# A five-layer decoder on one core: a table of step slots for each layer with projection halves apart, and the first batch requested ahead of the constant tables

## The reference, cut to what matters

```python
x = _layernorm(x + _L0_attn_ref(x, ...))            # layer 0: causal attention
x = _layernorm(x + _L0_xattn_ref(x, ctx, ...))      # layer 1: cross attention
x = _layernorm(x + _L0_ffn_ref(x, ...))             # layer 2: causal attention + 4 dense experts
x = _layernorm(x + _L1_attn_ref(x, ...))            # layer 3: attention with rotary positions
x = _layernorm(x + _L1_xattn_ref(x, ctx, ctx, group_prob, mask, ...))   # layer 4
x = _layernorm(x + _L1_ffn_ref(x, ...))             # top-1 routing to 8 experts
# in each attention layer:
q = h @ wq.T; k = h @ wk.T; v = h @ wv.T            # "projections"
scores = jnp.einsum('bhqd,bhkd->bhqk', q, k) * HD ** (-0.5)
attn = jax.nn.softmax(scores, axis=-1)
ao = jnp.einsum('bhqk,bhkd->bhqd', attn, v)
```

## Time and profile before

| | us |
|---|---|
| median of 3 runs | 1700.4 (1693.29 to 1702.75) |
| the profiled execution's own time | 1703.05 |
| its span, first to last instruction | 1701.3 |
| mean granted TensorE clock over the span | 0.941 of full |

### The profile page before, as it was taken

One profiled execution on the slowest core, in us unless ns is written; L12 is line 12 of the kernel. 1 busy time (PEld: TensorE's weight loads), 2 busy tenths in 40 slices (PEclk: granted clock), 3 DMA queues, 4 the chain that ended last, 5 costly groups with the idle time before them and its releaser, 6 DMA issues. The chain is left out here.

```text
span 1701.3 us, 29169 instructions
## 1 busy us (share of the span) xinstructions
PE 1514.3 (89%) x11260; PEld 1120.4 (66%) x11296; DVE 956.5 (56%) x2034; ACT 835.3 (49%) x1395; POOL 511.9 (30%) x690
## 2 busy tenths in 40 slices
PE   2799888988888999999999999987999999975997
PEld 2555655665555788787887877864655555545997
DVE  4455666755455342424335344367667788855886
ACT  0144445655444546455464564634543443435674
POOL 0024565531223111213223022033221223232766
PEclk9688989998888999999999999999999999987999
DMA  3645765755224021120210202223665354004542
GB/s 88 98 78 110 154 121 90 129 104 89 39 40 75 9 37 30 23 39 7 39 28 11 39 2 44 39 35 59 122 128 142 65 109 99 28 26 146 177 141 72
DMA packets 98745, 123.84 MB, mean 73 GB/s; under 512 B 8268, under 2 KB 88755, under 8 KB 96048
## 3 DMA queue, kind: packets, MB, share of 16 engines
q1 hardware_dynamic: 96096, 117.38, 35.1%
q0 software_dynamic: 1792, 3.94, 0.7%
q10 hardware_dynamic: 720, 0.66, 0.1%
HBM read 48.79 MB, written 9.51 MB: 34 GB/s over the span
## 5 line engine op out<-in xcount | busy, mean ns | idle before, releaser
L884 ACT ACTIVATE probs<-eslot 128x1024 f32<-128x1024 f32 x192 | 196.6, 1024 | 165.1 <-PE eslot L634 135.2
L1066 DVE TENSOR_REDUCE mx<-mslot 128x4 f32<-128x1024 f32 x128 | 156.5, 1223 | 155.4 <-PE mslot L608 154.9
L1302 POOL TENSOR_SCALAR_AFFINE_SELECT probs<-probs 128x512 f32<-128x512 f32 x128 | 83.4, 653 | 487.2 <-ACT probs L882 487.1
L1060 DVE TENSOR_REDUCE mx_blocks<-mslot 128x3 f32<-128x384 f32 x214 | 110.7, 551 | 193.9 <-PE mslot L608 182.4
L634 PEld LDWEIGHTS eslot<-stack 50*128 50x128 f32 (+1 forms) x1280 | 99.4, 192 | 119.1 <-issue 88.4
L634 PE MATMUL eslot<-stack 50*128 50x256 f32 (+2 forms) x1280 | 159.0, 328 | 17.2 <-ACT probs L884 9.6
L608 PE MATMUL mslot<-stack 48*128 48x256 f32 (+2 forms) x1110 | 142.2, 299 | 11.2 <-DMA stack<-split 9.6
L1274 POOL TENSOR_SCALAR ave<-amv 128x2 f32<-128x2 f32 x64 | 15.8, 247 | 432.2 <-DVE amv L983 342.6
L882 ACT ACTIVATE probs<-eslot 128x512 f32<-128x512 f32 (+1 forms) x256 | 111.7, 490 | 57.9 <-PE eslot L634 56.8
L648 PE MATMUL bank<-probs,v 128*32 128x256 f32 (+1 forms) x2048 | 137.4, 387 | 1.5 <-issue 1.5
L931 ACT ACTIVATE o<-bank 128x256 f32<-128x256 f32 x160 | 61.5, 384 | 115.3 <-PE bank L648 87.2
(11 more groups left out here) (226 smaller groups left out, 3381.7 us busy)
## 6 DMA issues: line engine op xcount, KB each, us to landing
stack<-split SPq DMA_DIRECT2D x240, 256.0 KB
w<-in_w SPq DMA_DIRECT2D x16, 1024.0 KB, 5.3
slot_rows<-hTf SPq DMA_DIRECT2D x4, 650.0 KB, 8.8
slot_rows_sb<-slot_rows SPq DMA_DIRECT2D x4, 650.0 KB, 6.3
expert_rows<-slot_rows SPq DMA_DIRECT2D x8, 260.0 KB, 2.8
xb<-in_x SPq DMA_DIRECT2D x8, 256.0 KB, 9.1
l<-in_l SPq DMA_DIRECT2D x2, 1024.0 KB, 9.0
qk<-in_ctx SPq DMA_DIRECT2D x8, 256.0 KB, 5.7
```

The costliest lines, as they stand in the source:

```text
L884: e = act.activation(PR[:, k, :, :, :].rearrange("p a k q -> p (a k q)"), ps[:, :, :, :].rearrange("p a k q -> p (a k q)"), ACT.Exp, scale ...
L1060: m = dve.tensor_reduce(MC[:, :, a, p], ps[:, 0:3 * P].rearrange("p (n k) -> p n k", k=P), AX.X, ALU.max)
L1066: dve.tensor_reduce(MX[:, :, :, p].rearrange("p q a -> p a q"), MSLOT[0][:, :, :].rearrange("p a (q k) -> p a q k", q=TT), AX.X, ALU.max)\
L1302: pool.affine_select(diagonal, diagonal, [[0, 2 * TT], [1, P]], ALU.is_ge, 0.0, base=0, channel_multiplier=-1)\
```

## The change

Four things are changed.

The table has new slots. The two halves of a projection, which stood in one slot in all layers, stand in different slots for `q` in layers 0, 2 and 3 and for `k` in layer 3. Of layer 0, `q` moves from -10 to -11, `q end` from -10 to -9 and `norm` from 28 to 32. Of layer 1, `H` moves from -13 to -15, `mask row` from -6 to -9, `xb` from -9 to -7, `y0` from 21 to 20. Of layer 2, `T` moves from -19 to -17 and `q end` from -16 to -15, `spread` from -11 to -10, `split` from -9 to -8, `yT` from 23 to 24, `route` from 29 to 30, `normf` from 37 to 38. Of layer 3, `T` moves from -19 to -17, `q end` to -15, `k end` to -13, `xb` from -10 to -13, `split` from -9 to -8, `stack` from -6 to -5, `v end` to -3, `yT` to 22, `w` from 26 to 24, `norm` to 30. Of layer 4, `keys` moves from -14 to -16, `masks` from -12 to -15, `turn masks` from -5 to -7, `stack` from -6 to -7, `xb` from -9 to -6, `v` from -3 to -4, `v end` to -2, `group` from 5 to 3, `scatter` from 38 to 35, `out` to 40. `H` of layers 2 and 3 stays at -20.

```diff
-        {"T": -13, "q": -10, "q end": -10, "k": -8, "k end": -8, "stack": -6, "v": -4, "v end": -4,
-         "shift": 8, "y0": 21, "y1": 21, "yT": 23, "w": 26, "w end": 26, "norm": 28},
+        {"T": -13, "q": -11, "q end": -9, "k": -8, "k end": -8, "stack": -6, "v": -4, "v end": -4, "shift": 8,
+         "y0": 21, "y1": 21, "yT": 22, "w": 26, "w end": 26, "norm": 32},
...
     EXP_LAG = (11, 11, 11, 11, 11)
-    MIX_LAG = (2, 1, 2, 1, 1)
+    MIX_LAG = (1, 1, 1, 1, 1)
```

```diff
+    EARLY = [(cols, "cols"), (tokens, "tokens"), (rope_cos, "rope_cos"), (rope_sin, "rope_sin"), (rope_swap, "rope_swap")]
+    SMALL = [(head_sum, "head_sum"), (head_spread, "head_spread"), (gate, "gate"), (prefer, "prefer"), (prefer_e, "prefer_e"),
+             (wg, "wg")]
...
         @block.sync
         def _(sp):
-            sp.dma_start(Y[:, 0, 0:P], t["causal_q"]).then_inc(consts_in, 16)
-            sp.dma_start(Y[:, 0, P:2 * P], t["upto"]).then_inc(consts_in, 16)
-            for dst, name in CONSTS:
-                sp.dma_start(dst.ap(), t[name]).then_inc(consts_in, 16)
-            sp.wait_ge(consts_in, 16 * (len(CONSTS) + 2))
+            sp.dma_start(X[0], t["x"][0:1].rearrange(flat)).then_inc(*x_in[0]())
+            sp.dma_start(ident[:, :], t["ident"]).then_inc(ident_in, 16)
+            for kind in "qkv":
+                sp.dma_start(WEIGHT_OF[kind][:, :, :], t["proj"][:, PROJ[kind](0), :, :]).then_inc(*weight_in[kind](0))
+            sp.dma_start(rows[:, 0, :], t["rows"][:, VROW[0], :]).then_inc(*row_in[0](0))
+            sp.wait_ge(ident_in, 16)
+            sp.wait_ge(consts_in, 16 * (len(EARLY) - 1))
+            sp.wait_ge(small_in, 16 * len(SMALL))
+
+        @block.scalar
+        def _(act):
+            act.dma_start(Y[:, 0, 0:P], t["causal_q"]).then_inc(tables_in, 16)
+            act.dma_start(Y[:, 0, P:2 * P], t["upto"]).then_inc(tables_in, 16)
+            for dst, name in EARLY:
+                act.dma_start(dst.ap(), t[name]).then_inc(tokens_in if name == "tokens" else consts_in, 16)
+            act.wait_ge(ident_in, 16)
+            act.activation(ident_b[:, :], ident[:, :], ACT.Copy)
 
         @block.gpsimd
         def _(pool):
+            for dst, name in SMALL:
+                pool.dma_start(dst.ap(), t[name]).then_inc(small_in, 16)
...
-            for k in range(RING):
-                dve.memset(QKS[k][:, :, 0, :].bitcast(F32), 1.0)
-                for a in range(2):
-                    dve.memset(QKS[k][HALF * a + 32:HALF * a + HALF, :, 1, :].bitcast(F32), 1.0)
+            for k in range(2):
+                dve.memset(QKS[k][:, :, :, :].bitcast(F32), 1.0)
...
             elif step == "k":
+                if l in (0, 2, 3):
+                    pe.wait_ge(*act_read.at("T", u))
                 project("k", u, source(u), 0)
...
+        pool.memset(QKS[2][:, :, :, :].bitcast(F32), 1.0).then_inc(*stack_ones(2))
```

More of the change, by code:

```diff
@@ L123, in schedule @@
     PLACE = (
-        {"T": -13, "q": -10, "q end": -10, "k": -8, "k end": -8, "stack": -6, "v": -4, "v end": -4,
-         "shift": 8, "y0": 21, "y1": 21, "yT": 23, "w": 26, "w end": 26, "norm": 28},
-        {"context": -17, "context sums": -14, "H": -13, "centre": -13, "T": -12, "TC": -11, "q": -10, "q end": -10, "mask": -10,
[11 rows of a table removed]
-         "turn masks": -5, "v": -3, "v end": -3, "group": 5,
-         "shift": 8, "y0": 21, "y1": 21, "yT": 23, "w": 26, "w end": 26, "norm": 28, "even": 30, "xT": 30, "even rows": 31,
-         "logits": 32, "chances": 33, "rank": 34, "scatter": 38, "out": 38},
+        {"T": -13, "q": -11, "q end": -9, "k": -8, "k end": -8, "stack": -6, "v": -4, "v end": -4, "shift": 8,
+         "y0": 21, "y1": 21, "yT": 22, "w": 26, "w end": 26, "norm": 32},
+        {"context": -17, "H": -15, "context sums": -14, "centre": -13, "T": -12, "TC": -11, "q": -10, "mask": -10,
+         "q end": -10, "mask row": -9, "k": -8, "k end": -8, "xb": -7, "stack": -6, "v": -4, "v end": -4, "shift": 8,
[7 rows of a table added]
+         "norm": 30},
+        {"keys": -16, "masks": -15, "T": -13, "q": -10, "q end": -10, "k": -8, "k end": -8, "turn masks": -7,
+         "stack": -7, "xb": -6, "v": -4, "v end": -2, "group": 3, "shift": 8, "y0": 21, "y1": 21, "yT": 23, "w": 26,
+         "w end": 26, "norm": 28, "even": 30, "xT": 30, "even rows": 31, "logits": 32, "chances": 33, "rank": 34,
+         "scatter": 35, "out": 40},
     )
     EXP_LAG = (11, 11, 11, 11, 11)
-    MIX_LAG = (2, 1, 2, 1, 1)
+    MIX_LAG = (1, 1, 1, 1, 1)
     for u in range(UNITS):
@@ L303, in attention_layers @@
     consts_in = semaphore("consts_in")
+    ident_in = semaphore("ident_in")
+    tokens_in = semaphore("tokens_in")
+    tables_in = semaphore("tables_in")
+    small_in = semaphore("small_in")
+    stack_ones = signal("stack_ones")
     experts_in = semaphore("experts_in")
@@ L330, in shift_rows @@
         return first, first + SHIFT
-    CONSTS = [(ident, "ident"), (rope_swap, "rope_swap"), (head_sum, "head_sum"), (head_spread, "head_spread"), (rope_cos, "rope_cos"),
-              (rope_sin, "rope_sin"), (cols, "cols"), (gate, "gate"), (prefer, "prefer"), (prefer_e, "prefer_e"), (wg, "wg"),
-              (tokens, "tokens")]
+    EARLY = [(cols, "cols"), (tokens, "tokens"), (rope_cos, "rope_cos"), (rope_sin, "rope_sin"), (rope_swap, "rope_swap")]
+    SMALL = [(head_sum, "head_sum"), (head_spread, "head_spread"), (gate, "gate"), (prefer, "prefer"), (prefer_e, "prefer_e"),
+             (wg, "wg")]
     EXPERTS = [(up0, "up0"), (l1, "l1"), (l2.ap(), "l2"), (downs, "downs"), (down3.ap(), "down3"), (l3.ap(), "l3"),
                (up3, "up3"), (up1a, "up1a"), (up1b.ap(), "up1b")]
+    flat = "b p t c -> (b p) t c"
     with nc.Block() as block:
@@ L364, in _ @@
             dve.memset(CLEAR[:, TOKEN:WIDE], 1.0)
-            dve.wait_ge(consts_in, 16 * (len(CONSTS) + 2))
+            dve.wait_ge(tokens_in, 16)
             for b in range(B):
@@ L368, in _ @@
                 dve.memset(XR[b][:, :, TOKEN + 1:WIDE], 0.0)
+            dve.wait_ge(tables_in, 32)
             dve.tensor_copy(upto_b[:, :], Y[:, 0, P:2 * P])
-            dve.tensor_copy(ident_b[:, :], ident[:, :])
             dve.tensor_copy(causal_q[:, :], Y[:, 0, 0:P])
@@ L1390, in stack @@
                 sp.wait_ge(*exp_filled.at(u - RING, PAIRS - 1))
+            elif u == 2:
+                sp.wait_ge(*stack_ones.at(2))
             for j, (a, b) in enumerate(zip(Q_PARTS, K_PARTS)):
@@ L1431, in reload @@
             sp.dma_start(WEIGHT_OF[kind][:, :, :], t["proj"][:, PROJ[kind](l), :, :]).then_inc(*weight_in[kind](l))
-        sp.dma_start(X[0][:, :, :], t["x"][0:1].rearrange(flat)).then_inc(*x_in[0]())
-        for kind in "qkv":
-            reload(kind, 0)
         reload("w", 1)
-        reload_row(0, 0)
         reload_row(1, 1)
```

1 line of the change is left out of this document (removed), and 18 rows, old and new, of the table PLACE.

## The result

The changed kernel takes 1602.15 us (median; 1590.84 to 1603.82), the kernel before 1697.41 us in the same comparison. The ratio is 0.9427 with a 95% interval of 0.938 to 0.9474: 5.7% faster, 95 us by the medians.

The account below looks back on a forecast made before the run. PE was taken as the bound, busy 89% of the span, with idle waits and a lowered clock in three stretches. Terms -13 - 14 - 28 - 10 + 5 = -60 took 1703.05 to 1643 us, range 1612 to 1686.

Parts of the forecast that it names:

- the clock term: PE work lost at 1.2 GHz: 6 of 25.1 us back in layer 0, 15 of 26.6 between layers 1 and 2, 3 of 8.7 in layer 3.
- The opening, -13: Kernel start: fewer DVE memsets and requests on POOL let PE start at 11.6 to 12.5 us, not 25.53; 13 us saved.
- Layer 0, -14: Layer 0: query bank read one slot later, after the `stack` landing; 8 us of idle time and 6 of clock saved.
- The limit that I saw close by: Layer 0: five slots from `stack` to the next query bank read, transfers 13 us, so 8 slots take at least about 21 us.
- Layers 1 to 2, -28: Between layers 1 and 2: later `T` removes PE's 12.9 us of waits for POOL's h, plus 15 us of clock.
- Layer 3, -10: Layer 3: `parts` before `split` saves 7 of 10.5 us of PE's waits, plus 3 us of clock.
- the waits only move on: Rival, all three turns: next limits close behind bring the old waits back; about -21 us, 1682 us; chance 0.22.
- Layers 2 and 4, 0: Layer 2's own 545 us stretch and layer 4, where PE is nearly always busy: no change, 0 us.
- What may cost, +5: Layers 0 and 2: `MIX_LAG` 1 leaves one slot for POOL's clearing between `exp` and `mix`; 5 us lost over 64 mixes.
- The rival in which POOL gates `mix`: Layers 0 and 2: POOL's 2.44 us blocks delay PE, 78 us in place of 5; 1716 us; chance 0.05.
- the one in which DVE's memsets hold up POOL's requests: Opening: POOL's six requests wait until 10.2 us, PE starts at 21, gain 4.5, and waits move; 1699 us; chance 0.03.
- more than forecast: Rival, whole kernel: waits gone and clock at 2.4 GHz throughout; -13 - 29 - 39 - 19 = -100, 1603 us; chance 0.07.

## Why the prediction was right and wrong

The direction, the places and, but for one in layer 3, the mechanisms held; the sizes did not, and they erred on one side. The step that failed is the idle time of PE, of which the sum counted too little; the clock term, though wrongly reasoned, was nearly right in size.

Between the two profiled executions 112 us went, where the sum had 60. Of these, 47 are PE's busy time and 65 its idle time; the sum had 24 (6, 15 and 3) for the clock and 36 for the rest (13, 8, 12.9 and 7, less 5). But the two lie apart on the clock. By the prediction's own sum, (1 - clock) x span, the clock gave back 100.4 - 46.1 = 54 us between them, and 91.6 - 62.5 = 29 us between executions near the medians (0.946 over 1696 us and 0.961 over 1602; an estimate). So of the 95 us by the medians the clock has about 29, and its term of 24 was nearly right. The idle time has the miss of some 29 us: 40 us in the three stretches where the sum had 28 less 5, 11 us in layers 2 and 4 (13.6 to 9.8 and 14.5 to 7.6) where it had nothing, and 1.4 us more in the opening.

*The opening, -13.* Measured -14.4 at PE's first product (25.53 to 11.11), a little beyond the bound "nothing lets it exceed 14", and -16.6 on the time of the whole kernel. I had taken 2.23 us for 2048 elements with the gap behind each of nine memsets and doubled it; the double-sized ones start 4.27 us apart. POOL's plain requests took about 0.55 us, near the lower bound, and x, landed 3.1 us after its request, did not wait for the weights (4.2 to 5.9 us).

*Layer 0, -14.* Measured -29 between the profiles: idle time by 10.9 where I had 8, busy time by 18 where I had 6. The waits for `parts` went from 9.0 to 2.8 us, and those for ACT's exponentials, of which I had counted little, from 6.5 to 0.8. The limit that I saw close by was wrong: "from `stack` to the next unit's read of the query bank there are now five slots ... so 8 slots cannot take much under 13 / 5 x 8 = 21 us". That took all slots for equally long. The five are those with `T`, `v`, the outputs and the query projection in them; they take 13.3 of the 19.5 us. With the halves together and the old lag the units reached 19 us, and there ACT's waits for the landing come back in part (2.9 us in two). Some of the term is chance of the profiled execution of before: four other executions with the same layer 0 steps took 184.0, 184.6, 185.3 and 187.8 us for the stretch, not 192.7, with 26 to 34 us at 1.2 GHz and not 49. Against their mean of 185 the gain is 22; the moved read gave 15 of it, close to the term, and the rest lies in units 5 to 8, where the cause is open.

*Layers 1 to 2, -28.* Measured -33: idle time by 17 where I had 12.9, busy time by 17 where I had 15. Of the time at 1.2 GHz 45 of 52 us went. `T` by itself took about 20 us off this stretch, and the rest came with the other moves of the table.

*Layer 3, -10.* Measured -16: idle time by 12.2 where I had 7, busy time by 5 where I had 3. I had reasoned from `split` alone, and that alone was worth little (-5.8 us for layers 2 and 3), because the wait moved to ACT: the rival "the waits only move on" was right for this one edit. What I had left out is that `q end` moved with it; with all of row 3 PE waited no more for `parts` and 3.0 us for the exponentials. That `q end` is the one that did it is argued from the 3.61 us row: it was not moved by itself.

*The clock.* I counted back a quarter, a bit over half and a third of what it cost in the three stretches, "because the short waits for DVE's maxima remain". They do remain, up to 1.7 us each, and the clock stood at 0.97, 0.98 and 0.99 in the profiled execution. There PE's busy time fell by 40 us for my 24, but 12 of the 16 us between lie in layer 0, with its chance, and the other executions of the changed kernel had a lower clock. The reason that I gave was wrong, for the stretch of 287 to 348 us in the kernel before had shown a clock of 1.00 with 3 us of gaps in 61; the size was nearly right.

*Layers 2 and 4, 0.* -6 and -7 us. Layer 4's row is the cause of its part: the halves of `v` are one piece of it, since with them together the stretch took 227 us. I had costed halves apart only as a bank held longer. In layer 2 some 3 us are the move of `T` in layer 3, whose first transposes lie in this stretch: PE's idle time there was 13.5 to 14.0 us in the five kernels that keep it and 10.7 to 11.1 in the three that move it and leave the rest of row 2 but `T` and `split` alone. The remainder stays open; the stretch took 534 to 549 us in the fourteen profiled executions.

*What may cost, +5.* The waits for POOL's clearing were 5.6 us over all of the kernel, 5 times. Right in size, and small beside the rest. The rival in which POOL gates `mix` and the one in which DVE's memsets hold up POOL's requests did not come about: six requests ran between 1.35 and 4.84 us beside DVE's first memset.

The rival "more than forecast" gave 1603 us, and 1602 was measured; but it has 39 us for layers 1 to 2 and 29 for layer 0 with the clock at 2.4 GHz throughout, and nothing for layers 2 and 4. That it met the number is in part luck.

## What to carry to other kernels

Where queues are in order, ask of each wait what stands behind it on its engine, and move the waiting step one slot behind the arrival of what it waits for; one such read was worth 17 us and one such transpose, moved in two layers, 32. When a step is moved, look for who shares a buffer with it and move that reader or writer too, or the wait comes back on another engine. Add up all of an engine's idle time in a stretch, not only the waits that have a name: here 40 us went where the named waits gave 28. And before a clock term is read from two profiles, set their mean clocks beside those of the other executions: here that halved it, from 54 to 29 us.

## What the runs showed of the hardware

The granted clock of the same instructions differs between executions: layer 0 with unchanged steps spent 26, 27, 27, 34 and 49 us at 1.2 GHz in five profiled ones. Times of one kernel therefore spread by 0.8% (1590.84 to 1603.82 of the changed one), and a profile should be set against the median before a term is read from it. The longest single wait does not tell the clock either: with none over 2.2 us layer 0 of the kernel before spent 49 us at 1.2 GHz, while the kernel with `T` alone moved had none of it in four of the six units between layers 1 and 2, with a wait of 2.3 us among them. A plain transfer request cost POOL 0.54 to 0.74 us against 0.43 to 0.45 on SP in the changed kernel, and ran beside DVE's 3.47 us memset of 4096 elements a partition; the Trainium skill's "SBUF — State Buffer" says under "Who interferes with whom" that a vector operation with at most one SBUF input, outside the two-port modes, does not contend with GpSimd, and these rows agree.
